# Unread identity matmuls in front of 48 TensorE steps at the start and the end of a 16-item pipeline

## The chip, the cores and the metric

The kernel runs on one core of one Trainium2 chip. The metric is device time in microseconds of one launch; the times given are medians of several launches on the same chip.

## The reference

The input has 16 items of 256 tokens by 256 features and a context of 77 rows for each item. A first layer is a transformer block: RMS norm and self-attention with 16 heads of 16 features, RMS norm and cross-attention to the context, RMS norm and a gated MLP with 1024 inner features.

```python
residual = hidden_states
h = rmsnorm(hidden_states, sa_norm_w)
h = residual + attention(h, h, sa_wq, sa_wk, sa_wv, sa_wo)
residual = h
hn = rmsnorm(h, ca_norm_w)
h = residual + attention(hn, context, ca_wq, ca_wk, ca_wv, ca_wo)
residual = h
hn = rmsnorm(h, mlp_norm_w)
h = residual + mlp(hn, w_gate, w_up, w_down)
```

A second layer takes the result `h` as queries: both `h` and the context are layer-normed, attention over the context with one head follows, then a GELU layer of 4 features and back to 256, a layer norm, self-attention over its 256 rows, and a sum with two learned scales.

## The kernel before, in words

All five engines run their own program. An item is cut into steps (`T.sa` transposes the normed tokens, `qk.sa` and `v.sa` make queries, keys and values, `S.sa.0` to `S.sa.7` the scores for the row maxima, `maxT.sa` transposes the maxima, `E.sa.0` to `E.sa.7` the scores shifted by them, `pv.sa.0` to `3` the attended values, `wo.sa` the projection; the same with `ca` for cross-attention; `T.mlp`, `gu.0` to `7` and `dnp.0` to `7` for the MLP; then `nFT`, `nXT`, `sc`, `pT`, `h4`, `xT`, `s2`, `mT2`, `e2`, `u2`, `fT`, `f2` for the second layer). Products whose operands are split in a high and a low part (`float32r`) run as three matmuls (`product`, line 1112); transposes, `pv`, `sc`, `h4` and `u2` have plain float32 operands.

`ORDER` writes out by hand the order in which each engine issues its steps, once around for each turn `it`; `name@a` stands for item `it + a`. `run` goes through the turns: the first and the last are unrolled, the middle ones are a hardware loop. The items overlap by up to four turns on TensorE, so that in the middle steps of several items stand between each other, and at the start and the end they don't. An engine issues strictly in this order. Where a step needs another engine's result, it waits for a semaphore. Steps that occur once (`kt`, `kg`, `fc`, weight splits `ws`) are in the same lists and do something only for item 0.

PSUM holds two tiles `ring` (attention), two `mring` (MLP and second layer), `od` (attended values) and `down_ps` (sum of the MLP, and before that scratch for `kt` and `kg`). The lines that matter here:

- TensorE (PE): `transposed` (L1120), `qk`, `v`, `wo`, `gu` by `product` (L1112), `scores` (L1173), `maxT` (L1180), `shifted` (L1193), `pv` (L1207), `dnp` (L1240), `t_nF` and `t_nX` (L1250), `sc` (L1269, L1271), `gram` (L1290, step `kg`), `pT` (L1298), `h4` (L1308), `t_sides` (L1316, step `xT`), `s2` (L1323), `mT2` (L1330), `e2` (L1337), `u2` (L1345), `t_stack` (L1352, step `fT`), `f2` (L1361).
- ScalarE (ACT): `scale_forms` (L693, L694, step `kg`) reads the Gram products from `down_ps` and writes `forms`; `mix_hi` (L676, step `fc`); `norm` (L723) squares the tokens and sums them; `exps` (L776).
- VectorE (DVE): the row maxima of the scores (L959, L964), the low parts (L937, L950, L952), `xn` (L932).
- GpSimd (POOL): `rstd` (L555) and, for each item, the chain of small operations that ends in `sides` (L650).
- SP issues the DMAs, among them those that pack queries and keys (`pk_sa<-qkT`, L493).

The first `dnp` of item 0 and `guard_forms` on VectorE wait until `forms` is made.

Of the kernel before, what the change touches and what calls it, by code (L numbers as in the profile page):

```python
# [23 lines left out]
P = 128  # L24
# [37 lines left out]
        xs@-6 hi.6@-5 hi.7@-5  # L62
    """,
    "act": """
        hi.7@-2 aT.ca@-1 v.sa@1 nXT@-2 norm.mlp@-1 h1@0 norm.ca@0 mT2@-3 ws.5@5 ws.10@1 T.mlp@-1 v.ca@0 T.ca@0 kg@0 e2@-3 maxT.sa@1 norm.sa@2 gu.0@-1 gu.1@-1
        qk.ca@0 hi.0@-1 E.sa.0@1 ws.7@4 gu.2@-1 hi.1@-1 E.sa.1@1 fc@4 E.sa.2@1 ws.4@6 gu.3@-1 nFT@-2 E.sa.3@1 fT@-3 E.sa.4@1 E.sa.5@1 sce@-2 ws.6@5 E.sa.6@1
        E.sa.7@1 pT@-2 ws.2@8 T.sa@2 hi.2@-1 hi.3@-1 maxT.ca@0 h4@-2 ws.3@7 ws.8@2 gu.4@-1 ws.0@15 qk.sa@2 cT.ca@1 gu.5@-1 E.ca.0@0 ws.9@2 hi.4@-1 hi.5@-1
        E.ca.1@0 gu.6@-1 ws.1@13 kt@12 aT.sa@1 gu.7@-1 E.ca.2@0 E.ca.3@0 hi.6@-1 xT@-2
    """,
# [34 lines left out]
def users(engine, wanted):  # L104

    return [(step, ahead) for step, ahead in STEPS[engine] if wanted(step)]


RINGS = {
# [35 lines left out]
def build(nc, x, ctx, w, vecs, norm_w, fc1t, fc1b, w5, out):  # L145
    st = ExitStack()
    with st:
# [941 lines left out]
        def _(pe):  # L1089
            mm = nc.tensor.matmul  # L1090
            pe.wait_ge(s_cset, 2)

            def weights(n, name):

                if at_first(n):
                    pe.wait_ge(s_wlo, C * (W_ORDER.index(name) + 1))
# [16 lines left out]
                return last  # L1113

            def transposed(n, tag):
                pe.wait_ge(S[tag, "xn"].sem, S[tag, "xn"].at(n, QT))
                ps = mfill(n, "T", "mlp") if tag == "mlp" else fill(n, "T", tag)[:, 0, :]
                for c in range(C):
                    for q in range(QT):
                        last = nc.tensor.transpose(ps[:, c * T + q * P:c * T + (q + 1) * P], XN[tag][:, q, c * P:(c + 1) * P], ident[:])  # L1120
                last.then_inc(S[tag, "T"].sem, 1)
# [6 lines left out]
                last.then_inc(S["cTmm"].sem, 1)  # L1128

            def qk(n, tag):  # L1130
                pe.wait_ge(S[tag, "lo"].sem, S[tag, "lo"].at(n, 1))
                if tag == "ca":
                    pe.wait_ge(S["cTlo"].sem, S["cTlo"].at(n, 1))
                    if at_first(n):
                        pe.wait_ge(s_cset, 10)
                weights(n, f"{tag}_wk")
                ps = fill(n, "qk", tag)
                wq, wk = wt[f"{tag}_wq"], wt[f"{tag}_wk"]
                src, kw = (hT_a, T) if tag == "sa" else (cT, SKV2)
                for m in range(C):  # L1140
                    product(ps[:, 0, m * T:(m + 1) * T], lambda a, kc: wq[a][:, kc, m * P:(m + 1) * P], lambda b, kc: hT_a[b][:, kc, :], C)
                for m in range(C):
                    last = product(ps[:, 1, m * kw:(m + 1) * kw], lambda a, kc: wk[a][:, kc, m * P:(m + 1) * P], lambda b, kc: src[b][:, kc, :], C)
                last.then_inc(S[tag, "qkmm"].sem, 1)

            def v(n, tag):
                if tag == "ca":
                    pe.wait_ge(S["cTlo"].sem, S["cTlo"].at(n, 1))
                weights(n, f"{tag}_wv")
                ps = fill(n, "v", tag)  # L1150
                wv = wt[f"{tag}_wv"]
                for q in range(QT if tag == "sa" else 1):
                    if tag == "sa":
                        last = product(ps[:, 0, q * D:(q + 1) * D], lambda a, kc: hT_a[a][:, kc, q * P:(q + 1) * P], lambda b, kc: wv[b][:, kc, :], C)
                    else:
                        last = product(ps[0:SKV, 0, 0:D], lambda a, kc: cT[a][:, kc, 0:SKV], lambda b, kc: wv[b][:, kc, :], C)
                last.then_inc(S[tag, "vmm"].sem, 1)

            def scores(n, tag, k):

                c, i0, pairs = pair_head(k, tag)
                if k == 0:
                    pe.wait_ge(S[tag, "pk0"].sem, S[tag, "pk0"].at(n, 16 * PACKS[tag][0]))
                if tag == "sa" and k == 4:
                    pe.wait_ge(S[tag, "pk1"].sem, S[tag, "pk1"].at(n, 16 * PACKS[tag][1]))
                ps = fill(n, "S", tag, k)
                kw = KW[tag]
                for i in range(pairs):
                    for q in range(QT):
                        for half in range(2):  # L1170
                            col = (i * QT + q) * kw
                            slot, r = SLOT_AT[tag](c, i0 + i), slice(HALF * half, HALF * half + MAX_ROW)
                            last = mm(ps[:, half, col:col + kw], qpk[tag][r, slot, q * P:(q + 1) * P], kpk[tag][r, slot, :], start=True, stop=True)  # L1173
                last.then_inc(S[tag, "S"].sem, 1)

            def maxT(n, tag):
                pe.wait_ge(S[tag, "nm"].sem, S[tag, "nm"].at(n, 1))
                ps = fill(n, "maxT", tag)
                for q in range(QT):
                    last = nc.tensor.transpose(ps[0:2 * SLOTS, 0, q * P:(q + 1) * P], nm[tag][:, q].rearrange("p h s -> p (h s)"), ident[:])  # L1180
                last.then_inc(S[tag, "maxT"].sem, 1)

            def shifted(n, tag, k):

                c, kt, i0, g = shifted_at(k, tag)
                if k == 0:
                    pe.wait_ge(S[tag, "mr"].sem, S[tag, "mr"].at(n, 16))
                ps = fill(n, "E", tag, k)
                rows_ = P if tag == "sa" else SKV
                for u in range(2):  # L1190
                    for half in range(2):
                        slot, r = SLOT_AT[tag](c, i0 + u), slice(HALF * half, HALF * (half + 1))
                        last = mm(ps[0:rows_, half, u * T:(u + 1) * T], kpk[tag][r, slot, kt * P:kt * P + rows_], qpk[tag][r, slot, :], start=True, stop=True)  # L1193
                last.then_inc(S[tag, "E"].sem, 1)

            def pv(n, tag, g):

                rows_, tiles = (P, QT) if tag == "sa" else (SKV, 1)
                c, kt = g // tiles, g % tiles
                pe.wait_ge(S[tag, "exp"].sem, S[tag, "exp"].at(n, 2 * (g + 1)))  # L1200
                if g == 0:
                    pe.wait_ge(S[tag, "vz"].sem, S[tag, "vz"].at(n, 1))
                if kt == 0:
                    reuse(pe, "od", ("pv", tag, g), n)
                for half in range(2):
                    for i in range(PAIRS):
                        last = mm(od[32 * i:32 * i + 32, half, :], vz[tag][0:rows_, kt, 8 * c + 2 * i + half, :], granule(g, tag)[0:rows_, i, half, :],  # L1207
                                  start=(kt == 0 and half == 0), stop=(kt == tiles - 1), tile_position=(0, 32 * i), skip_group_check=True)
                last.then_inc(S[tag, "pv"].sem, 1)

            def wo(n, tag):
                pe.wait_ge(S[tag, "athi"].sem, S[tag, "athi"].at(n, 1))
                pe.wait_ge(S[tag, "atlo"].sem, S[tag, "atlo"].at(n, 1))
                weights(n, f"{tag}_wo")
# [3 lines left out]
                last.then_inc(S[tag, "wo"].sem, 1)  # L1218

            def gu(n, m):  # L1220
                if m == 0:
                    pe.wait_ge(S["mlp", "lo"].sem, S["mlp", "lo"].at(n, 1))
                    weights(n, "up")
# [68 lines left out]
                    last.then_inc(s_gram, 1)  # L1292

            def pT(n):
                pe.wait_ge(S["lp"].sem, S["lp"].at(n, QT))
                ps = mfill(n, "pT")
                for q in range(QT):
# [1 line left out]
                last.then_inc(S["pTmm"].sem, 1)  # L1299

            def h4(n):
                pe.wait_ge(S["lpT"].sem, S["lpT"].at(n, 1))
                pe.wait_ge(S["xf"].sem, S["xf"].at(n, 1))
                if at_first(n):
# [4 lines left out]
                last.then_inc(S["h4"].sem, 1)  # L1309

            def t_sides(n):
                pe.wait_ge(S["xs"].sem, S["xs"].at(n, 7))
                ps = mfill(n, "xT")
                for side in range(2):
# [2 lines left out]
                last.then_inc(S["xT"].sem, 1)  # L1317

            def s2(n):
                pe.wait_ge(S["xTe"].sem, S["xTe"].at(n, 1))  # L1320
                ps = mfill(n, "s2")
                for q in range(QT):
# [1 line left out]
                last.then_inc(S["s2"].sem, 1)  # L1324

            def mT2(n):
                pe.wait_ge(S["smx"].sem, S["smx"].at(n, 1))
                ps = mfill(n, "mT2")
                for q in range(QT):
# [1 line left out]
                last.then_inc(S["mT2"].sem, 1)  # L1331

            def e2(n):
                pe.wait_ge(S["shift"].sem, S["shift"].at(n, 1))
                ps = mfill(n, "e2")
                for kt in range(QT):
# [59 lines left out]
```

## Time and profile before

| | us |
|---|---|
| median of 3 runs | 1021.01 (1020.12 to 1021.73) |
| the profiled execution | 1021.97 |
| its span, first to last instruction | 1020.2 |
| PE busy | 899.7 (88%), 8142 matmul records |
| DVE busy | 672.6 (66%) |
| ACT busy | 546.0 (54%) |
| POOL busy | 261.6 (26%) |
| chain that ended last, by engine | PE 77%, DVE 12%, issue 4%, ACT 3% |
| mean granted clock of TensorE | 0.937 |

Times in the profile are microseconds from the span's first instruction. PE is TensorE's matmuls, PEld its weight loads. `MATMUL ring<-hT_a_hi,sa_wq_hi` writes `ring` from the two operands; `128*128 128x256` has 128 rows and 128 columns of weights and 256 moving columns. A record's duration includes the way through the array, so neighbouring records overlap, and the distance from start to start is what one takes of the engine's time. In a merged row, the time runs from the first start to the last end.

### The profile page before, as it was taken

Reading aid. Unit: us, or ns where it says so; the run is one execution under the profiler, and the core shown is the slowest. Engines: PE = TensorE matmul, PEld = TensorE weight load, DVE = VectorE, ACT = ScalarE, POOL = GpSimd, SP = SyncE. Lnnn points to the kernel's source line nnn. Section 1 sums busy time; section 2 is a strip of 40 time slices with the busy share of each in tenths; the row PEclk is TensorE's granted clock in tenths of the full one; section 3 lists DMA queues with packets and bytes.
Section 4 is the critical chain, followed back from the end, with each engine's and each line's share of the span. In section 5 each row is a group of like instructions: output and inputs, shape, how many; then the busy total and the mean of one; then the engine's idle time right before and its main releaser. Section 6 shows DMA issues by size and latency. Waiting matters only on the chain.

```text
span 1020.2 us, 21920 instructions
## 1 busy us (share of the span) xinstructions
PE 899.7 (88%) x8142; PEld 762.2 (75%) x8142; DVE 672.6 (66%) x1439; ACT 546.0 (54%) x1129; POOL 261.6 (26%) x547
## 2 busy tenths in 40 slices
PE   3565879999999999999999999999999999989784
PEld 3434657788787888887878888788888787878673
DVE  4436284958677786959595867677685959564531
ACT  3332345455656657474656565655647475655342
POOL 7000001113232322222222323232322222233242
PEclk9766689999999999999999999999999999989895
DMA  6302121212222212021122221222213111201000
GB/s 186 120 13 75 53 79 53 80 52 69 64 77 66 77 59 85 26 97 44 54 80 64 80 63 66 65 76 65 76 28 106 33 59 63 65 4 53 4 11 21
DMA packets 69266, 63.97 MB, mean 63 GB/s; under 512 B 17280, under 2 KB 64496, under 8 KB 69184
## 3 DMA queue, kind: packets, MB, share of 16 engines
q1 hardware_dynamic: 69184, 62.87, 19.3%
q8 instruction: 53, 0.87, 0.4%
q14 instruction: 29, 0.24, 0.1%
HBM read 16.55 MB, written 4.19 MB: 20 GB/s over the span
## 4 chain that ended last, share of the span: by engine, by line
PE 77%; DVE 12%; issue 4%; ACT 3%; DMA 2%; POOL 1%; SPq 1%; DVEq 0%; POOLq 0%; ACTq 0%
PE mring L1112 18%; PE ring L1112 17%; PE down_ps L1240 10%; PE od L1207 10%; PE ring L1193 6%; PE ring L1173 6%; DVE mx_sa L959 5%; PE ring L1120 2%; DVE xn_a L932 2%; PE mring L1345 1%; PE mring L1269 1%; PE mring L1316 1%; PE mring L1308 1%; DVE xn_m L932 1%; DVE mx_ca L964 1%
## 5 line engine op out<-in xcount | busy, mean ns | idle before, releaser
L776 ACT ACTIVATE probs<-ring 128x1024 f32<-128x1024 f32 (+1 forms) x192 | 191.8, 1020 | 42.7 <-PE ring L1193 37.5
L559 POOL TENSOR_TENSOR hidT_lo<-hid,hidT_hi 128x256 fp32r<-128x256 f32 x128 | 94.7, 749 | 377.2 <-ACT hidT_hi L799 376.7
L959 DVE TENSOR_REDUCE mx_sa<-ring 128x4 f32<-128x1024 f32 x128 | 152.8, 1218 | 13.8 <-PE ring L1173 13.5
L1008 DVE SCALAR_TENSOR_TENSOR hid<-hid,mring 128x256 f32<-128x256 f32 x128 | 53.1, 415 | 90.8 <-ACT hid L791 90.4
L1173 PE MATMUL ring<-pk_sa 63*128 63x256 f32 x512 | 61.7, 341 | 27.7 <-DVE mx_sa L959 11.8
L1240 PE MATMUL down_ps<-down_hi,hidT_hi 128*128 128x256 f32 x256 | 80.0, 312 | 0.0
L1173 PEld LDWEIGHTS ring<-pk_sa 63*128 63x128 f32 x512 | 40.3, 201 | 47.1 <-DVE mx_sa L959 15.6
L975 DVE STREAM_TRANSPOSE oS<-od 128x512 f32<-128x512 f32 x64 | 45.7, 714 | 44.5 <-PE od L1207 43.9
L1207 PE MATMUL od<-probs,vz_sa 128*32 128x256 f32 x1024 | 72.0, 400 | 1.2 <-DVE oS L975 0.5
L1240 PE MATMUL down_ps<-down_lo,hidT_hi 128*128 128x256 f32 x256 | 72.6, 284 | 0.0
L1240 PE MATMUL down_ps<-down_hi,hidT_lo 128*128 128x256 f32 x256 | 72.5, 283 | 0.0
L791 ACT ACTIVATE hid<-mring 128x256 f32<-128x256 f32 x128 | 48.2, 380 | 40.6 <-PE mring L1112 39.6
L964 DVE TENSOR_REDUCE mx_ca<-ring 128x4 f32<-128x308 f32 x128 | 53.8, 474 | 18.2 <-PE ring L1173 16.8
L1193 PE MATMUL ring<-pk_sa 64*128 64x256 f32 x512 | 60.2, 335 | 5.3 <-DMA pk_sa<-mT 2.5
L799 ACT ACTIVATE hidT_hi<-hid 128x256 fp32r<-128x256 f32 x128 | 49.7, 410 | 28.1 <-PE down_ps L1240 27.2
L1112 PE MATMUL mring<-hT_m_hi,gate_hi 128*128 128x256 f32 x256 | 59.8, 316 | 2.4 <-DVE hT_m_lo L937 1.1
L950 DVE TENSOR_TENSOR qkT<-ring,qkT 128x512 fp32r<-128x512 f32 x32 | 22.1, 692 | 58.8 <-ACT qkT L749 58.8
L749 ACT ACTIVATE qkT<-ring 128x512 fp32r<-128x512 f32 x32 | 19.1, 598 | 72.1 <-PE ring L1112 72.1
L1193 PEld LDWEIGHTS ring<-pk_sa 64*128 64x128 f32 x512 | 39.5, 200 | 24.1 <-ACT probs L776 8.1
L1240 PEld LDWEIGHTS down_ps<-down_hi,hidT_hi 128*128 128x128 f32 x256 | 48.8, 191 | 10.9 <-POOL hidT_lo L559 6.2
L1010 DVE SCALAR_TENSOR_TENSOR hid<-hid,mring 128x256 f32<-128x256 f32 x128 | 53.9, 421 | 4.4
L732 ACT ACTIVATE hT_a_hi<-ring 128x512 fp32r<-128x512 f32 x32 | 19.1, 598 | 63.6 <-PE ring L1120 63.6
(278 smaller groups left out, 2424.6 us busy)
## 6 DMA issues: line engine op xcount, KB each, us to landing
pk_sa<-qkT SPq DMA_DIRECT2D x96, 256.0 KB, 2.7
qpk_ca<-qkT SPq DMA_DIRECT2D x48, 256.0 KB, 2.6
x_sb<-x SPq DMA_DIRECT2D x16, 256.0 KB, 2.8
x_res<-x SPq DMA_DIRECT2D x16, 256.0 KB, 2.7
out<-o_sb SPq DMA_DIRECT2D x16, 256.0 KB, 2.2
kpk_ca<-qkT SPq DMA_DIRECT2D x48, 78.0 KB, 2.1
ctx_sb<-ctx SPq DMA_DIRECT2D x16, 77.0 KB
ctx_l<-ctx SPq DMA_DIRECT2D x16, 77.0 KB
```

What stands on the lines that cost most here:

```text
L559: nc.gpsimd.tensor_tensor(hidT[1][:, m % HID, :], hid[:, m % 2, :], hidT[0][:, m % HID, :].bitcast(F32), ALU.subtract).then_inc(S["hidlo"] ...
L776: nc.scalar.activation(granule(g, tag)[0:rows_, i0:i0 + 2, :, :].rearrange("p i h t -> p h i t"), ring_tile(("E", tag, k))[0:rows_].rearra ...
L799: nc.scalar.activation(hidT[0][:, m % HID, :], hid[:, m % 2, :], ACT.Copy).then_inc(S["hidhi"].sem, 1)
L959: nc.vector.tensor_reduce(mx[tag][:, :, :, k].rearrange("p q h -> p h q"), ps[:].rearrange("p h (q t) -> p h q t", t=T), AX_X, ALU.max).th ...
L964: nc.vector.tensor_reduce(mx[tag][:, :, half, 2 * C * (k % 2) + k // 2:2 * C * (k % 2) + k // 2 + C + 1:C].rearrange("p q i -> p i q"), v, ...
L1008: nc.vector.scalar_tensor_tensor(out=hid[:, m % 2, :], in0=hid[:, m % 2, :], scalar=1.0, in1=ps[:, 0:T], op0=ALU.add, op1=ALU.mult).then_i ...
L1010: nc.vector.scalar_tensor_tensor(out=hid[:, m % 2, :], in0=hid[:, m % 2, :], scalar=0.5, in1=ps[:, T:2 * T], op0=ALU.mult, op1=ALU.mult).t ...
L1112: last = mm(outs, left(a, k % chunks), right(b, k % chunks), start=(k == 0), stop=(k == total - 1))
L1173: last = mm(ps[:, half, col:col + kw], qpk[tag][r, slot, q * P:(q + 1) * P], kpk[tag][r, slot, :], start=True, stop=True)
L1193: last = mm(ps[0:rows_, half, u * T:(u + 1) * T], kpk[tag][r, slot, kt * P:kt * P + rows_], qpk[tag][r, slot, :], start=True, stop=True)
L1207: last = mm(od[32 * i:32 * i + 32, half, :], vz[tag][0:rows_, kt, 8 * c + 2 * i + half, :], granule(g, tag)[0:rows_, i, half, :], start=(k ...
L1240: last = mm(down_ps[:, q, :], hidT[a][:, m % HID, q * P:(q + 1) * P], wt["down"][b][:, m, :], start=(m == 0 and q == 0 and k == 0), stop=( ...
```

## The change

`SPIN` is a table from a step and its item to a count. In front of each of these 48 steps, TensorE issues as many matmuls of the 128x128 float32 identity with itself; nothing reads the result. For items below 8 they write to the first 128 columns of `down_ps` and wait until `forms` is made; for the later items they write to `od` and wait until the last attended values are read. 310 of the 464 stand in front of 31 steps of items 0 to 2, 154 in front of 17 steps of items 13 to 15. Only unrolled turns hold them. The wait and the spins of a step come before the step's own wait. On ScalarE, `kg` moves from turn 0 to turn -4, right behind `fc`.

```diff
     "act": """
-        hi.7@-2 aT.ca@-1 v.sa@1 nXT@-2 norm.mlp@-1 h1@0 norm.ca@0 mT2@-3 ws.5@5 ws.10@1 T.mlp@-1 v.ca@0 T.ca@0 kg@0 e2@-3 maxT.sa@1 norm.sa@2 gu.0@-1 gu.1@-1
-        qk.ca@0 hi.0@-1 E.sa.0@1 ws.7@4 gu.2@-1 hi.1@-1 E.sa.1@1 fc@4 E.sa.2@1 ws.4@6 gu.3@-1 nFT@-2 E.sa.3@1 fT@-3 E.sa.4@1 E.sa.5@1 sce@-2 ws.6@5 E.sa.6@1
+        hi.7@-2 aT.ca@-1 v.sa@1 nXT@-2 norm.mlp@-1 h1@0 norm.ca@0 mT2@-3 ws.5@5 ws.10@1 T.mlp@-1 v.ca@0 T.ca@0 e2@-3 maxT.sa@1 norm.sa@2 gu.0@-1 gu.1@-1
+        qk.ca@0 hi.0@-1 E.sa.0@1 ws.7@4 gu.2@-1 hi.1@-1 E.sa.1@1 fc@4 kg@4 E.sa.2@1 ws.4@6 gu.3@-1 nFT@-2 E.sa.3@1 fT@-3 E.sa.4@1 E.sa.5@1 sce@-2 ws.6@5 E.sa.6@1
...
+SPIN = {
+    ("T.sa", 0): 19, ("qk.sa", 0): 11, ("S.sa.0", 0): 48, ("v.sa", 0): 16, ("S.sa.4", 0): 13, ("S.sa.6", 0): 7, ("S.sa.7", 0): 10,
+    ("maxT.sa", 0): 11, ("E.sa.0", 0): 19, ("E.sa.2", 0): 4, ("pv.sa.2", 0): 3, ("qk.sa", 1): 13, ("S.sa.0", 1): 39, ("wo.sa", 0): 7,
+    ("S.sa.4", 1): 13, ("S.sa.6", 1): 6, ("v.ca", 0): 2, ("maxT.sa", 1): 3, ("qk.ca", 0): 2, ("E.sa.1", 1): 6, ("E.sa.3", 1): 4,
+    ("S.ca.2", 0): 4, ("T.sa", 2): 3, ("qk.sa", 2): 6, ("E.ca.0", 0): 9, ("E.ca.2", 0): 6, ("E.ca.3", 0): 2, ("wo.ca", 0): 4, ("S.sa.6", 2): 4,
+    ("v.ca", 1): 5, ("S.ca.0", 1): 11, ("T.mlp", 15): 31, ("gu.0", 15): 7, ("gu.2", 15): 3, ("fT", 13): 6, ("pT", 14): 6, ("e2", 14): 7,
+    ("u2", 14): 10, ("fT", 14): 4, ("pT", 15): 4, ("h4", 15): 2, ("xT", 15): 43, ("s2", 15): 4, ("mT2", 15): 6, ("e2", 15): 3, ("u2", 15): 7,
+    ("fT", 15): 8, ("f2", 15): 3,
+}
...
+            def spin(n, *step):
+
+                count = SPIN.get((".".join(map(str, step)), n), 0) if isinstance(n, int) else 0
+                if count and n < B // 2:
+                    pe.wait_ge(s_form, 2)
+                elif count:
+                    pe.wait_ge(S["ca", "o"].sem, S["ca", "o"].at(B - 1, 2))
+                for _ in range(count):
+                    mm(down_ps[:, 0, 0:P] if n < B // 2 else od[:, 0, 0:P], ident[:], ident[:], start=True, stop=True)
...
             def transposed(n, tag):
+                spin(n, "T", tag)
                 pe.wait_ge(S[tag, "xn"].sem, S[tag, "xn"].at(n, QT))
```

The other step functions begin with the same call.

## Rows read from the trace of the kernel before

**Rows 1.** Page part 2: tenths in 40 slices of 25.5 us.

```profile
PE   3565879999999999999999999999999999989784
...
PEclk9766689999999999999999999999999999989895
```

**Rows 2.** Windows: stretch, its us, busy us (x instructions) of each engine, PEclk, DMA share, GB/s.

```profile
26.00:168.20 142.20, 99.08 (x717) 74.27 (x718) 70.65 (x109) 54.69 (x96) 6.08 (x9) 0.75 0.22 69
952.60:1016.90 64.30, 42.00 (x252) 36.85 (x252) 20.16 (x63) 23.02 (x52) 21.47 (x53) 0.74 0.03 10
```

**Rows 3.** Timeline of PE, three steps with long waits: start, us, work, [idle before <-releaser].

```profile
40.29 1.22 PE L1173 MATMUL ring<-pk_sa 63*128 63x256 f32 x8 [6.18 <-DMA pk_sa<-qkT]
...
956.58 1.11 PE L1120 MATMUL mring<-ident,xn_m 128*128 128x128 f32 x4 [4.01 <-DVE xn_m L932]
...
1005.26 1.12 PE L1316 MATMUL mring<-ident,sides 128*65 128x128 f32 x4 [5.47 <-POOL sides L650]
```

**Rows 4.** Timeline of PE, `qk` of items 0 and 1, line 1112.

```profile
29.21 0.63 PE L1112 MATMUL ring<-hT_a_lo,sa_wq_hi 128*128 128x256 f32 x2
...
33.48 0.63 PE L1112 MATMUL ring<-hT_a_hi,sa_wk_lo 128*128 128x256 f32 x2
...
73.62 0.41 PE L1112 MATMUL ring<-hT_a_lo,sa_wq_hi 128*128 128x256 f32 x2
...
76.00 0.40 PE L1112 MATMUL ring<-hT_a_hi,sa_wk_lo 128*128 128x256 f32 x2
```

**Rows 5.** Windows of seven stretches of the first part and three of the tail, with sums.

```profile
26.03:34.20 8.17, 6.57 (x28) 5.91 (x28) 0.69 (x1) 2.72 (x4) 0.00 (x0) 1.00 0.00 0
...
133.10:140.20 7.10, 7.10 (x52) 4.50 (x51) 6.03 (x8) 1.84 (x3) 0.00 (x0) 0.52 0.59 179
...
sum 80.67, PE 61.37 PEld 45.28 DVE 33.47 ACT 24.84 POOL 2.07; mean PE 8.77 PEld 6.47 DVE 4.78 ACT 3.55 POOL 0.30
...
sum 37.20, PE 22.42 PEld 18.74 DVE 6.97 ACT 12.70 POOL 9.01; mean PE 7.47 PEld 6.25 DVE 2.32 ACT 4.23 POOL 3.00
```

**Rows 6.** Groups by form, whole span (busy, mean ns); then timeline of one group each.

```profile
L1120 PE MATMUL ring<-ident,xn_a 128*128 128x128 f32 x128 | 22.4, 303 | 13.8 <-DVE xn_a L932 12.8 <-DVE mx_ca L964 0.6 <-ACT vz_ca L759 0.3
...
L1269 PE MATMUL mring<-nXT,nFT 128*128 128x77 f32 x128 | 17.3, 281 | 0.0
...
970.22 1.09 PE L1269 MATMUL mring<-nXT,nFT 128*128 128x77 f32 x8
...
312.21 0.60 PE L1120 MATMUL mring<-ident,xn_m 128*128 128x128 f32 x4
```

**Rows 7.** Timeline of PE and ScalarE at the start, and the forms' activation.

```profile
18.25 5.26 PE L1290 MATMUL down_ps<-w6T 128*128 128x5 f32 x24
26.03 1.11 PE L1120 MATMUL ring<-ident,xn_a 128*128 128x128 f32 x4 [2.51 <-DVE xn_a L932]
...
19.88 0.42 ACT L676 ACTIVATE mix<-o_sb 40x256 fp32r<-40x256 f32 x1 [2.31 <-POOL o_sb L601]
20.20 0.40 ACT L723 ACTIVATE xn_a<-x_sb 128x256 f32<-128x256 f32 x1
...
99.81 0.19 ACT L693 ACTIVATE forms<-down_ps 128x25 f32<-128x25 f32 x1
```

**Rows 8.** Timeline of PE around a rise and a fall of the clock.

```profile
66.52 1.93 PE L1207 MATMUL od<-probs,vz_sa 128*32 128x256 f32 x16
...
69.39 1.07 PE L1207 MATMUL od<-probs,vz_sa 128*32 128x256 f32 x16 [0.49 <-DVE oS L975]
...
84.72 0.77 PE L1112 MATMUL ring<-sa_wo_hi,atT_hi 128*128 128x256 f32 x2 [0.99 <-DVE mx_sa L959]
...
89.03 0.40 PE L1112 MATMUL ring<-sa_wv_lo,hT_a_hi 128*128 128x256 f32 x2
...
92.64 1.22 PE L1173 MATMUL ring<-pk_sa 63*128 63x256 f32 x8 [1.79 <-DVE mx_sa L959]
```

**Rows 9.** Page part 5: the exps of the softmax.

```profile
L776 ACT ACTIVATE probs<-ring 128x1024 f32<-128x1024 f32 (+1 forms) x192 | 191.8, 1020 | 42.7 <-PE ring L1193 37.5
```

More of the change, by code:

```diff
@@ L1130, in qk @@
             def qk(n, tag):
+                spin(n, "qk", tag)
                 pe.wait_ge(S[tag, "lo"].sem, S[tag, "lo"].at(n, 1))
@@ L1146, in v @@
             def v(n, tag):
+                spin(n, "v", tag)
                 if tag == "ca":
@@ L1159, in scores @@
             def scores(n, tag, k):
+                spin(n, "S", tag, k)
                 c, i0, pairs = pair_head(k, tag)
@@ L1176, in maxT @@
             def maxT(n, tag):
+                spin(n, "maxT", tag)
                 pe.wait_ge(S[tag, "nm"].sem, S[tag, "nm"].at(n, 1))
@@ L1183, in shifted @@
             def shifted(n, tag, k):
+                spin(n, "E", tag, k)
                 c, kt, i0, g = shifted_at(k, tag)
@@ L1211, in wo @@
             def wo(n, tag):
+                spin(n, "wo", tag)
                 pe.wait_ge(S[tag, "athi"].sem, S[tag, "athi"].at(n, 1))
@@ L1220, in gu @@
             def gu(n, m):
+                spin(n, "gu", m)
                 if m == 0:
@@ L1294, in pT @@
             def pT(n):
+                spin(n, "pT")
                 pe.wait_ge(S["lp"].sem, S["lp"].at(n, QT))
@@ L1301, in h4 @@
             def h4(n):
+                spin(n, "h4")
                 pe.wait_ge(S["lpT"].sem, S["lpT"].at(n, 1))
@@ L1311, in t_sides @@
             def t_sides(n):
+                spin(n, "xT")
                 pe.wait_ge(S["xs"].sem, S["xs"].at(n, 7))
@@ L1319, in s2 @@
             def s2(n):
+                spin(n, "s2")
                 pe.wait_ge(S["xTe"].sem, S["xTe"].at(n, 1))
@@ L1326, in mT2 @@
             def mT2(n):
+                spin(n, "mT2")
                 pe.wait_ge(S["smx"].sem, S["smx"].at(n, 1))
@@ L1333, in e2 @@
             def e2(n):
+                spin(n, "e2")
                 pe.wait_ge(S["shift"].sem, S["shift"].at(n, 1))
@@ L1340, in u2 @@
             def u2(n):
+                spin(n, "u2")
                 pe.wait_ge(S["sp2"].sem, S["sp2"].at(n, 1))
@@ L1348, in t_stack @@
             def t_stack(n):
+                spin(n, "fT")
                 pe.wait_ge(S["fs"].sem, S["fs"].at(n, 2))
@@ L1355, in f2 @@
             def f2(n):
+                spin(n, "f2")
                 if at_first(n):
```

1 line of the change is left out of this document (added).

## The prediction

> **What bounds the kernel now.** I read the page first, then the stretches by their sums, then TensorE's instructions in order of time. The page's 40 slices show TensorE (PE) busy for nine tenths or more in the middle, and less in the first six slices and in some of the last four, where the granted clock is lower too [rows 1]. PE is the engine that holds most of the chain that ended last. In between nothing changes by this diff, so the argument is about two stretches: from the first transpose of item 0 at 26.0 us to the first cross-attention scores of item 1 at 168.2 us, and from 952.6 us to the last matmul. PE is busy 99.08 of 142.2 us in the one and 42.00 of 64.3 us in the other, so it waits 43.1 and 22.3 us [rows 2]. The order of its steps is fixed, and its longest waits are 6.18 us for the packing DMAs of item 0, 5.47 for the GpSimd chain to `sides` of item 15 and 4.01 for `xn_m` [rows 3].
>
> The second loss is the clock. The column of the granted clock says 1.00 from 26.03 to 34.20 [rows 5], yet there 20 matmuls of 256 columns start 0.2135 us apart (29.21 to 33.48), and the same step for item 1 starts 20 of them in 2.38 us, 0.119 apart [rows 4]. The spacings are the two levels, 1.2 and 2.4 GHz; where column and spacing differ I go by the spacing. By it the level was low in seven stretches of the first part, with 61.37 us of busy PE, and in three of the tail, with 22.42 us [rows 5].
>
> **What a spin costs.** Each is a float32 matmul, 128x128 weights, 128 moving columns, not a transpose. Lines 1269 and 1120 tell what that makes: `sc` issues 4 such matmuls for each of 16 items and has 128 records, two for each; the transposes of line 1120 are 8 for each item and also have 128, one for each [rows 6]. So 464 spins are 928 records. Three rows bound one record at the high level. L1269 (weight load of 128 columns, short moving side) takes 1.09 us for 8: with a last one of 0.28 (the mean) that is 0.116 apart. Four transposes (128 moving columns, identity) take 0.60; with the same last one they are about 0.109 apart [rows 6]. L1112, which has a full load and as long a stream, gives 0.119 [rows 4]. I take 0.119 as a spin has both sides full: 0.238 us for a spin, 0.427 at the low level. The bounds are 0.218 and 0.238. This is what decides the case: the count in the table is the wait divided by half of that. `S.sa.0` of item 0 waited 6.18 us and gets 48 spins, `xT` of item 15 waited 5.47 and gets 43, `T.mlp` 4.01 and 31 [rows 3]: nine tenths of the wait at 0.115 to 0.116 each, one record. At 0.238 they take 11.4, 10.2 and 7.4 us. PE is in order, so what a spin takes beyond the wait delays the step.
>
> The Trainium skill (TensorE: Matmul & The Clock Gate, "Back-to-back issue gap") has about 81 ns for a sustained pair of load and matmul of 128 columns; by an estimate from that page a spin would be 0.162 us and the sum about 34 us lower. The float32 pairs of this trace do not agree with it, so the rows stand.
>
> **The sum, part by part.**
>
> *Forms moved up.* The first spin waits for the two activations of `forms`, which start at 99.81 us now, so the diff moves `kg` on ScalarE to just behind `fc` (19.88) and ahead of the norm of item 0 (20.20) [rows 7]. There it waits for the Gram products, which end at 23.51, and takes 0.3: the squares begin near 23.9, 3.7 later. Queued behind them are the mean square on VectorE, the power on GpSimd, `xn` and the transpose, which was at 26.03 and now could start at 29.7. Nothing else on ScalarE wants that time, and SP's and GpSimd's queues issue in the same order. PE meanwhile runs 19 spins from 24.0. At the low level all take 8.1 us (end 32.1), at the high 4.5 (end 28.5, the data then decide). The level had risen by 89.03, 4.3 us after the unbroken work of 84.72 had begun, but not in the 4.3 us from 29.21 to 33.48 [rows 4, 8]. I take the rise after 6 us: 14 low, 5 high, end 31.2. **+5.2** (bounds +3.7 and +6.1).
>
> *Clock.* From then on PE hardly pauses, and work that now runs low should run high: 61.37 us x (1 - 0.119/0.2135) = 0.443 gives **-27.2**, and in the tail 22.42 x 0.443 = **-9.9**.
>
> *Spins in place of waits.* In the first stretch 291 spins ahead of 30 steps (the 19 apart): 69.3 us, for 43.1 us of wait of which 2.0 stay as they are, so **+28.2**. In the tail 154 spins ahead of 17 steps: 36.7 for 22.0 of 22.3, **+14.7**.
>
> *Ends.* A step in front of a wait shows its last matmul in full, 0.28 against a spacing of 0.12 [rows 6]; a spin follows without that. 30 and 17 x 0.16: **-4.8** and **-2.7**.
>
> *New waits.* With PE faster, the exps at 1.02 us each [rows 9] set the pace of eight E steps of items 0 and 1, where PE has some 7.7 us of work and spins for 8.5 to 9; `S.sa.3` waits 0.5 for `vz`, and `maxT` of item 1 about 1 for its maximum. **+4**, and +0.5 in the tail (bounds 0 and 8). Packing DMAs and maxima stay under the spins: 11.4 us lie over the 6.18.
>
> Other additions: the waits on `s_form` and on `oS` of item 15 are met when reached (nothing, covered by program order); two writes to `down_ps` or `od` fall where these are free. 1,856 more records are instructions to fetch, none seen to stall PE: 0, at most 1.
>
> First stretch +5.4, tail +2.6, together **+8.0**. The middle is taken as unchanged, with up to 3 either way, since its few low stretches may fall otherwise. On the profiled execution (1021.97 around a span of 1020.2; 0.96 above the median) this is 1030.0; on the median 1021.01 it is **1029.0**.
>
> **Rivals.**
>
> *Cheap spins, the other side.* The gain of 44.6 us from clock and ends stands; only the price eats it. At 445 spins the break-even is 0.238 - 8.0/445 = 0.220 us. Place: the 48 in front of `S.sa.0` of item 0 and the 43 in front of `xT`. At 0.218 and with no new waits: 8.0 - 8.9 - 4.5 = -5.4, about 1015.6. For it: the transposes' stream is as long. Against: their weight load is shorter. 0.13. If a spin were one record, its time would fit the waits, spins would add nothing: start 3.7, -27.2 - 9.9 + 4.5 = -29, about 992. The record counts speak against it: 0.04. The page's 81 ns would give about 995; 0.02 for that.
>
> *Level falls in the thin parts.* It was high at 89.03 and low again by 92.64, with PE waiting 1.79 us just before [rows 8]. If the new waits near `maxT` of item 1 or in the E steps do that, two falls like the low stretch from 133.1 us, whose 7.10 us of work [rows 5] x 0.443 is 3.1, cost 6: 1035. 0.10.
>
> *The level does not rise for spins.* Then 445 x (0.427 - 0.238) = +84 and the 37 of gain are lost, and work that is now high turns low in part: above 1150. Against it, the rise between the two groups of `od` matmuls at 66.52 (1.93 us for 16) and 69.39 (1.07) came in the midst of float32 matmuls [rows 8]. 0.03. The Trainium skill (same page, Part 4) says that transposes by TensorE don't bring the full clock as they don't count as busy in the same way; a product of the identity with itself is computed as a plain matmul, and no row here shows one.
>
> *The diff does nothing,* its matmuls dropped as unread: no row speaks for it, under 0.01.
>
> **How the numbers follow.** Forecast's own case 0.56 (1023 to 1041), falls 0.10, no rise 0.03: slower 0.69. Within 2 us either way, where price and new waits lie between the bounds: 0.12. Cheap spins in their three forms: faster 0.19. 0.2%, 2 us, is about what a measurement of this kernel can tell from none. The range leaves out 992 to 995, the no-rise case and what lies beyond the outer bounds: 1014 to 1041.
>
> **What would show it.** Right: a spin group with two records for each, 0.237 us a spin; `S.sa.0` of item 0 preceded by 96 records over 11 us and no idle; `xT` of item 15 starting some 3 us later behind the last `h4` than now (5.47 to over 9.5); matmuls of L1112 at 0.119 from about 31 us on; item 0's transpose near 31; `forms` near 24. Wrong: 464 records, spins of 0.12, PE idle ahead of the spun steps, or spacings of 0.2135 in the midst of them.

## The result, and the profile after

The changed kernel takes 1028.16 us (median of 20 runs, 1027.51 to 1030.21), the kernel before on the same chip 1022.97 (20 runs, 1018.96 to 1027.77). The ratio is 1.0047, 95% interval 1.0032 to 1.0061: slower, by about half a per cent. The forecast was 1029.0. The profiled execution has a span of 1026.4 us against 1020.2, 6.2 longer.

The page of the changed kernel, parts 1 and 2 (cut), answers to [rows 1]:

```profile
PE 968.4 (94%) x9070; PEld 841.2 (82%) x9070; DVE 672.0 (65%) x1439; ACT 545.2 (53%) x1129; POOL 261.5 (25%) x547
...
PE   4999999999999999999999999999999999989998
...
PEclk9999999999999999999999999999999999999999
```

Every slice but the first and two near the end is now nine tenths full, and the mean granted clock is 0.992, for 0.937 before: what is left at the low level is TensorE's work up to 27.7 us (by its spacings; the column shows 1.00 there) and five short stretches in the middle. By busy share and clock this looks like an ideal kernel, and it is slower than before. What fills the waits of both ends is line 1112, the spins. Their instructions in the changed kernel (durations are min/median/max):

```profile
L1112 PE MATMUL down_ps<-ident x620: 270/275/579, 24.1 to 174.2; 128*128 128x128 f32 x155
...
L1112 PE MATMUL od<-ident x308: 270/275/357, 957.2 to 1022.4; 128*128 128x128 f32 x154
```

620 + 308 = 928 records for 464 spins: two for each. The windows of the changed kernel, from the first transpose of item 0 to the first cross-attention scores of item 1, and from the first `smax` transpose of the tail's first step to the end of the last matmul (columns as in [rows 2]; there the tail's window begins behind the same `smax` step, which starts at 952.19 in the kernel before and has 0.38 us of work):

```profile
30.13:174.39 144.26, 139.60 (x1301) 121.75 (x1300) 70.34 (x109) 53.89 (x94) 6.08 (x9) 1.00 0.22 69
...
957.02:1022.98 65.96, 65.58 (x565) 63.88 (x563) 20.41 (x63) 23.20 (x52) 21.41 (x53) 1.00 0.03 11
```

The waits are nearly gone: 144.26 - 139.60 = 4.66 us are left in the first stretch and 0.38 in the tail, for 43.1 and 22.3 before [rows 2]. Yet both stretches are longer. TensorE in order of time, changed kernel:

```profile
24.09 6.20 PE L1112 MATMUL down_ps<-ident 128*128 128x128 f32 x38 [0.37 <-ACT forms L705]
30.13 0.60 PE L1142 MATMUL ring<-ident,xn_a 128*128 128x128 f32 x4
...
35.63 0.40 PE L1133 MATMUL ring<-hT_a_hi,sa_wk_lo 128*128 128x256 f32 x2
35.86 10.88 PE L1112 MATMUL down_ps<-ident 128*128 128x128 f32 x96
46.67 0.73 PE L1198 MATMUL ring<-pk_sa 63*128 63x256 f32 x8
47.33 3.84 PE L1112 MATMUL down_ps<-ident 128*128 128x128 f32 x32
...
53.71 3.17 PE L1112 MATMUL down_ps<-ident 128*128 128x128 f32 x26
56.81 0.74 PE L1198 MATMUL ring<-pk_sa 63*128 63x256 f32 x8
...
957.24 7.08 PE L1112 MATMUL od<-ident 128*128 128x128 f32 x62
964.16 0.60 PE L1142 MATMUL mring<-ident,xn_m 128*128 128x128 f32 x4
...
1003.40 9.85 PE L1112 MATMUL od<-ident 128*128 128x128 f32 x86
1013.08 0.60 PE L1349 MATMUL mring<-ident,sides 128*65 128x128 f32 x4
```

`S.sa.0` of item 0 waited 6.18 us; now 96 records stand there for 10.8. `T.mlp` waited 4.01 and has 6.9 in its place; `xT` waited 5.47 and has 9.7 [rows 3]. No bracket with a releaser stands behind the steps that follow: their data were there before the spins ended. 95 spacings in 10.88 - 0.28 us are 0.112 each, so within a group a spin costs 0.223 us, against 0.115 in the table's sizes. A short group costs more: the 13 spins from 53.71 to 56.81 take 3.10 us, 0.238 each. Record by record, where a group stands behind matmuls with 63 or 64 rows or 32 columns of weights (23 of the 30 in the first stretch), the last of these keeps TensorE for 0.2 us or more before the first spin's record starts, and that record for 0.213.

The ledger, from the starts of the same steps in both traces:

| stretch | forecast | measured | of which |
|---|---|---|---|
| start, to `T.sa` of item 0 | +5.2 | +4.1 | 26.03 to 30.13 |
| first stretch | +0.2 | +2.1 | work -28.1, spins for waits +30.2 |
| middle | 0, 3 either way | -1.4 | |
| tail | +2.6 | +1.4 | work -11.5, spins for waits +12.9 |
| sum | +8.0 | +6.2 | |

To divide a stretch, each matmul record counts from its start to the start of the next one, or to its own end where TensorE then idles. In the first stretch the 582 spin records behind the first 38 count 68.7 us (0.236 for each spin); the waits fell by 43.1 - 4.66 = 38.4, which leaves +30.2. The rest of busy TensorE is 139.60 - 68.7 = 70.9, for 99.1 before. In the tail, 308 records count 34.7 us (0.226 for each spin) in place of 21.8 us of waits (22.2 - 0.4), and the rest fell from 42.4 to 30.8.

So two large terms of opposite sign stand against each other, and three theories could be had from the start. **Theory P (price):** the clock and the filled waits are worth some 25 to 35 us; each spin costs two records where the counts assume one, and that eats it all. **Rival R (no gain to have):** the spins bring nothing, or the moved forms are what costs. **Rival T:** what a spin must be, to hold the clock, is a plain matmul.

### The profile page after: what moved, and what is told of

Same layout as the page of the kernel before. It is cut to its first block, busy times and chain, and to the rows that moved or that the text cites. A ratio compares the mean times of both kernels' runs of the same rounds, so it can differ in the third digit from the quotient of the medians.

```text
span 1026.4 us, 23776 instructions
## 1 busy us (share of the span) xinstructions
PE 968.4 (94%) x9070; PEld 841.2 (82%) x9070; DVE 672.0 (65%) x1439; ACT 545.2 (53%) x1129; POOL 261.5 (25%) x547
## 4 chain that ended last, share of the span: by engine, by line
PE 86%; DVE 8%; issue 2%; ACT 1%; DMA 0%; POOL 0%; SPq 0%; DVEq 0%; ACTq 0%; POOLq 0%
PE mring L1133 19%; PE ring L1133 16%; PE down_ps L1270 10%; PE od L1235 9%; PE down_ps L1112 7%; PE ring L1220 6%; PE ring L1198 5%; DVE mx_sa L970 4%; PE od L1112 3%; PE ring L1142 2%; PE mring L1382 1%; PE mring L1299 1%; DVE xn_a L943 1%; PE down_ps L1320 1%; PE mring L1349 1%
## 5 line engine op out<-in xcount | busy, mean ns | idle before, releaser
L1112 PE MATMUL down_ps<-ident 128*128 128x128 f32 x620 | 78.4, 283 | 0.4 <-ACT forms L705 0.4
L1112 PEld LDWEIGHTS down_ps<-ident 128*128 128x128 f32 x620 | 73.3, 196 | 4.1 <-issue 1.2
L1235 PE MATMUL od<-probs,vz_sa 128*32 128x256 f32 x1024 | 68.5, 385 | 0.7
L1198 PE MATMUL ring<-pk_sa 63*128 63x256 f32 x512 | 57.9, 323 | 9.8 <-DVE h L1013 4.1
L1198 PEld LDWEIGHTS ring<-pk_sa 63*128 63x128 f32 x512 | 37.4, 187 | 27.5 <-DVE mx_sa L970 10.7
L1220 PE MATMUL ring<-pk_sa 64*128 64x256 f32 x512 | 57.2, 322 | 1.0 <-ACT probs L787 1.0
```

Of the source, the lines that this page charges most:

```text
L1112: mm(down_ps[:, 0, 0:P] if n < B // 2 else od[:, 0, 0:P], ident[:], ident[:], start=True, stop=True)
```

## The experiments

Each edit is against the changed kernel, and none changes what is computed. Each ratio is to runs of the kernel before on the same chip. `kg_only`, `half`, `transposes` and `half_kg2` ran on one chip; `two_halved`, `half_up`, `tail_only` and `early_spins` on a second; `half_shifted` and `early_19` on a third; `kg2_shifted` on a fourth. Between chips the ratios are the fairer comparison, and a difference of medians is only a rough one.

**The move of `kg` alone.** `SPIN` is emptied; the order on ScalarE is the changed one.

```diff
-SPIN = {
-    ("T.sa", 0): 19, ("qk.sa", 0): 11, ...
-}
+SPIN = {}
```

> The changed kernel with an empty SPIN table: only kg stands earlier on ScalarE. Theory (the price of the spins makes the loss, the early kg a part of it): the squares of item 0 begin 3.7 us later and the whole pipeline with them, so 2 to 4 us over the kernel before, clock low in the same places. Rival (the late start is hidden by the weight splits or DMAs): within 1 us of before.

Measured: 1024.36 us (12 runs), before 1021.82 (17 runs), ratio 1.0021, interval 0.9998 to 1.0044. The interval just reaches 1, so a loss in time is not settled by it. The delay at the start is in the timeline of TensorE:

```profile
29.67 1.12 PE L1134 MATMUL ring<-ident,xn_a 128*128 128x128 f32 x4 [5.66 <-DVE xn_a L935]
```

The transpose stood at 26.03 with a wait of 2.51 [rows 7] and stands at 29.67: 3.6 later, which is the 3.7 worked out for the squares queued behind `kg`. The span of this one execution is 2.3 longer; if that holds for the kernel, about 1.3 is made up later, but executions of one kernel differ by more than that. The other 0.5 of the changed kernel's 4.1 is the first spin group, which outlasts the data.

**Half the spins.** One edit tests the price: counts that a spin of 0.223 fills.

```diff
-                for _ in range(count):
+                for _ in range(count // 2):
```

> Each count of SPIN halved and rounded down, so that a group of records takes nine tenths of its wait at 0.113 us a record. Theory (a spin is two records of 0.113, what goes beyond the wait is the loss, and the clock's gain is whole): the 464 spins took 104 us in place of some 65 us of waits, so about 39 us less than the changed kernel, 2 of it lost to waits that come back: 991, between 985 and 998. Rival (the clock stays high only because the spins leave no gap): low stretches come back, 1000 to 1012. Rival (the loss has little to do with the price): above 1018.

Measured: 1001.18 us (4 runs), ratio 0.9789 (0.9759 to 0.982). Windows of this kernel, the first stretch and 7.7 us inside it:

```profile
105.80:113.50 7.70, 7.70 (x56) 5.90 (x55) 4.16 (x11) 1.02 (x1) 0.00 (x0) 0.50 0.00 0
29.11:155.96 126.85, 113.25 (x993) 91.79 (x994) 70.15 (x109) 53.95 (x94) 6.08 (x9) 0.96 0.24 78
```

The same spins, half as many, are worth 2.1% against before and some 26 us against the changed kernel (by the ratios 1.0047 and 0.9789). Rival R falls. But the gain is 10 us short of the 991 expected, and 1001.18 lies where the rival of returning low stretches was put (1000 to 1012). One such stretch is there: 7.70 us at the low level in the first window. What stands in front of it, on TensorE in this kernel:

```profile
104.95 0.92 PE L1198 MATMUL ring<-kpk_ca,qpk_ca 63*128 63x78 f32 x8 [1.92 <-DMA qpk_ca<-qkT]
105.80 1.93 PE L1235 MATMUL od<-probs,vz_sa 128*32 128x256 f32 x16
```

A wait of 1.92 us for a packing DMA, then the low clock. Two suspects for the missing 10 us follow: this wait with what hangs on it (1.92 and 7.70 x 0.443 = 3.4 us), and the waits that a count rounded down leaves open (126.85 - 113.25 = 13.6 us of idle in all). A third thing stands in the same window. Counted as above, TensorE's own work in the stretch is 74.3 us, for 99.1 before, but the waits, with the spins in them, are 39.0 + 13.6 = 52.6 us, for 43.1 before: the data come from other engines and DMAs, which did not get faster (VectorE is busy for 70.15 us in the window, 70.65 before), so part of what the clock saves turns into wait.

**Transposes in place of matmuls,** full counts: same operands, one record for each.

```diff
-                    mm(down_ps[:, 0, 0:P] if n < B // 2 else od[:, 0, 0:P], ident[:], ident[:], start=True, stop=True)
+                    nc.tensor.transpose(down_ps[:, 0, 0:P] if n < B // 2 else od[:, 0, 0:P], ident[:], ident[:])
```

> The full counts, but each spin a transpose of the identity (one record of 0.109 us) in place of a float32 matmul. Theory (TensorE's clock follows transposes as it follows matmuls): the same as the halved counts within 4 us, about 991. Rival, from the Trainium skill (TensorE: Matmul & The Clock Gate, Part 4: transposes don't bring the full clock): spacings of 0.2135 stay where they were low before, each spin takes 0.21 and 97 us of spins stand against 65 of waits: 1040 to 1060.

Measured: 997.41 us (4 runs), ratio 0.9755 (0.9724 to 0.9785). The spins and the steps behind them in this kernel:

```profile
24.07 4.32 PE L1112 MATMUL down_ps<-ident 128*128 128x128 f32 x19 [0.37 <-ACT forms L705]
29.36 0.66 PE L1142 MATMUL ring<-ident,xn_a 128*128 128x128 f32 x4 [0.97 <-DVE xn_a L943]
29.85 1.36 PE L1112 MATMUL down_ps<-ident 128*128 128x128 f32 x11
...
31.83 0.39 PE L1133 MATMUL ring<-hT_a_lo,sa_wq_hi 128*128 128x256 f32 x2
...
29.35:151.30 121.95, 109.15 (x1009) 86.84 (x1009) 70.07 (x109) 54.09 (x94) 6.08 (x9) 1.00 0.25 81
```

Nineteen spins are 19 records here, spaced by 0.109 at the high level, and the `qk` matmuls of item 0 run at the high level from 31.52 us, where they ran at the low one before [rows 4]. The change as it was sized fits this instruction. Rival T falls: a transpose brings and holds the high level as well. The same division of the first stretch into TensorE's work and its waits, for five kernels:

| us | length | work | spins | idle | spins and idle |
|---|---|---|---|---|---|
| before | 142.2 | 99.1 | 0 | 43.1 | 43.1 |
| changed kernel | 144.3 | 70.9 | 68.7 | 4.7 | 73.3 |
| `half` | 126.9 | 74.3 | 39.0 | 13.6 | 52.6 |
| `transposes` | 121.9 | 71.2 | 37.9 | 12.8 | 50.7 |
| `half_shifted` (below) | 121.8 | 71.2 | 38.0 | 12.7 | 50.7 |

The clock, with what the ends of the groups give, saves 28 us of work in three of them. Where the spins fit, 7.6 us of that come back as longer waits, and 20 are kept; in the changed kernel 30 come back.

**Half, with `kg` in another place:** behind the squares of item 0, so that they don't queue behind it.

```diff
-... fc@4 kg@4 E.sa.2@1 ...
+... fc@4 E.sa.2@1 ...
-... norm.sa@2 gu.0@-1 ...
+... norm.sa@2 kg@2 gu.0@-1 ...
```

> Halved counts and kg on ScalarE right behind the norm of item 0 (turn -2) rather than ahead of it. Theory (the late squares cost at the start): the first transpose comes near 27 in place of 30, and the whole is 2 to 4 us under the halved counts alone, about 988. Rival (start hidden): equal to it within 1 us.

Measured: 999.82 us (4 runs), ratio 0.9767 (0.9736 to 0.9798), 1.4 under `half` on the same chip, with ranges that just don't overlap. Less than expected: the transpose moved only from 29.11 to 28.10, since now the 18 records ahead of it hold it, and the wait of the cross-attention scores was there again, at 2.04 us, with low stretches from 60.4 and 108.2 us in this execution.

**The two largest counts alone:** 48 to 24 and 43 to 21.

```diff
-    ... ("S.sa.0", 0): 48, ...
+    ... ("S.sa.0", 0): 24, ...
-    ... ("xT", 15): 43, ...
+    ... ("xT", 15): 21, ...
```

> The changed kernel with only two counts cut: 48 to 24 ahead of S.sa.0 of item 0 and 43 to 21 ahead of xT of item 15. Theory (what one group takes beyond its wait goes to the end undiminished): 24 x 0.224 = 5.4 less 0.8 of wait that comes back, and 22 x 0.224 = 4.9 less 0.9: 8.6 under the changed kernel, 1019.6. Rival (an overrun is caught up by later slack): under 4 us.

Measured: 1020.78 us (12 runs), ratio 0.9987 (0.997 to 1.0005); 7.4 under the changed kernel by the medians and 6.1 by the ratios, for 8.6 expected. On TensorE in this kernel:

```profile
37.07 5.52 PE L1112 MATMUL down_ps<-ident 128*128 128x128 f32 x48
43.43 0.74 PE L1198 MATMUL ring<-pk_sa 63*128 63x256 f32 x8 [0.83 <-DMA pk_sa<-qkT]
...
1007.50 4.93 PE L1112 MATMUL od<-ident 128*128 128x128 f32 x42
1013.36 0.65 PE L1349 MATMUL mring<-ident,sides 128*65 128x128 f32 x4 [0.92 <-POOL sides L661]
```

The steps behind the spins have their releasers back, 0.83 us for the packing DMA and 0.92 for `sides`: the spins now end just ahead of the data. The traced execution is the slowest of the twelve, though (1028.48 us): its cross-attention scores of item 0 waited 1.60 us for a packing DMA, and a low stretch of 10.2 us followed. The two groups can be read from it, the total can't. 46 fewer of 464 spins turn the change from slower into no measurable difference. This is the most direct evidence for theory P.

**The tail alone,** with transposes as spins and `kg` back in its old turn (these two edits not shown).

```diff
-                count = SPIN.get(...) if isinstance(n, int) else 0
+                count = 0 if isinstance(n, int) and n < B // 2 else SPIN.get(...) if isinstance(n, int) else 0
```

> Transposes as spins only ahead of the 17 steps of the tail, kg back in its old turn. Theory: the first stretch as before, the tail 7.4 us shorter as in the run with transposes everywhere (57.2 against 64.6): about 1014.5 against 1022. Rival (the gains of the two ends are not independent): more than 2 us away from that.

Measured: 1014.07 us (10 runs), ratio 0.9946 (0.9918 to 0.9973). As expected: the tail alone gives 5.5 us (by the ratio) to 6.6 (by the medians) of the 24 of `transposes`.

**Half, rounded up.** The question was whether the short waits that rounding down leaves open matter, and whether the wait at 105 us returns.

```diff
-                for _ in range(count):
+                for _ in range((count + 1) // 2):
```

> Halved counts rounded up rather than down: 19 more matmuls in all, which also moves the 16 KB blocks in which TensorE's instructions are fetched. Theory (in the halved counts the packing DMAs of item 0's cross-attention landed after 4.4 us in place of 2.6 because such a block came at the same moment, at 101.6 us; the 1.92 us of wait let the clock fall for some 7 us): if the block falls elsewhere, the wait ahead of the first S.ca is 0.4 and the time 3 to 4 us less than the halved counts: 998. Rival (the wait belongs to the halved counts, whatever the blocks do): 1001 to 1003, the same wait of 1.9.

Measured: 997.81 us (4 runs), ratio 0.977 (0.9732 to 0.9807), 3.4 under `half` by the medians and 1.9 by the ratios, whose intervals overlap. In its trace the 1.92 us are gone:

```profile
104.36 0.64 PE L1198 MATMUL ring<-kpk_ca,qpk_ca 63*128 63x78 f32 x8 [0.35 <-ACT probs L787]
```

**What made that wait.** The DMAs that pack `qpk_ca` for item 0, in `half` and in `half_up`, from issue to landing:

```profile
DMA to landing us min/median/max: 2.9/3.1/4.4
...
q8 instruction: 1, 0.02, 0.8%
```

```profile
DMA to landing us min/median/max: 2.5/2.6/2.7
```

The second line of the first fence is from the queues of `half` between 99 and 106 us: one packet of the queue that fetches instructions, 16 KB, while the three packing DMAs are on their way. In `half_up` the same window has no such line. In four kernels (`half`, `half_kg2`, `two_halved`, `early_spins`) such a packet fell 1 to 2 us behind the last of the three issues, and the wait was 1.60 to 2.04 us; in the six others with spins in this stretch none fell there, and the wait was 0.34 or 0.35. To move only the packet, 24 unread matmuls were put ahead of TensorE's first step, where it waits anyway:

```diff
             pe.wait_ge(s_cset, 2)
+            for _ in range(24):
+                mm(down_ps[:, 0, 0:P], ident[:], ident[:], start=True, stop=True)
...
-                for _ in range(count):
+                for _ in range(count // 2):
```

> The halved counts (rounded down) with 24 more matmuls of the identity ahead of TensorE's first step, where it waits until 12.9 us anyway. They do nothing for the places of the waits, but they move TensorE's program by 96 instructions, 6 KB, so the 16 KB block that was fetched at 101.6 us comes some 5 us earlier. Theory (that block delayed the packing DMAs): the wait ahead of the first S.ca goes from 1.9 to 0.4 us and the low stretch behind it is gone: 997 to 998 in place of 1001.2. Rival (rounding up helped by its spins, the block is chance): wait 1.9, 1001.

Measured: 996.82 us (4 runs), ratio 0.9779 (0.9755 to 0.9802), before 1020.18. On TensorE:

```profile
103.78 0.64 PE L1200 MATMUL ring<-kpk_ca,qpk_ca 63*128 63x78 f32 x8 [0.34 <-ACT probs L787]
```

With the counts of `half`, the wait is gone and the median is 4.4 us lower, on another chip; by the ratios it is 1.0, which is not clear of noise. The trace is the surer witness: no packet falls among the three DMAs, and the first stretch is 121.8 us long for 126.9, 5.0 shorter, where the wait and the low stretch were priced at 5.3. `half_up`, with 122.9, is no shorter than this, so rounding down costs nothing here. So some kernels of this family carry up to 5 us in the first stretch that go with where their instruction blocks fall.

**Spins from the start.** On top of `transposes`, 70 more ahead of the first step, and 50 ahead of `T.sa` of item 0, were to bring the high level before the Gram products.

```diff
             pe.wait_ge(s_cset, 2)
+            for _ in range(70):
+                nc.tensor.transpose(down_ps[:, 0, 0:P], ident[:], ident[:])
...
-    ("T.sa", 0): 19, ...
+    ("T.sa", 0): 50, ...
```

> Transposes as spins, and 70 more before TensorE's first step, while it waits for the 12.9 us of masks and folding, and 50 in place of 19 ahead of T.sa of item 0. Theory (the early kg costs 3.3 us at the start because the Gram products run at the low clock until 23.5 and the squares wait for them): with the clock up they end near 18.9, before the squares are due at 20.2, so T.sa of item 0 starts near 26.1 as in the kernel before, 3.3 us under the run with transposes: 994. Rival (the clock falls during the Gram products, whose moving side has 5 columns): spacings of 0.2135 in them, T.sa near 29.5, the same time as with transposes.

Measured: 1002.53 us (4 runs), ratio 0.9802 (0.9761 to 0.9844): 8 us worse than expected, and 5 worse than `transposes`. The start in this kernel:

```profile
1.55 10.37 PE L1104 MATMUL down_ps<-ident 128*128 128x128 f32 x70 [1.55 <-POOL ident L536]
...
14.19 2.39 PE L1322 MATMUL down_ps<-wcT 128*128 128x5 f32 x20 [0.67 <-ACT w6T L697]
16.44 4.77 PE L1322 MATMUL down_ps<-w6T 128*128 128x5 f32 x24
21.58 8.41 PE L1114 MATMUL down_ps<-ident 128*128 128x128 f32 x50 [0.37 <-ACT forms L705]
29.83 0.60 PE L1144 MATMUL ring<-ident,xn_a 128*128 128x128 f32 x4
```

At the low level 70 records would take 69 x 0.2135 + 0.28 = 15.0 us; they took 10.37, so the level rose in the midst of transposes alone. It was still high for the first 20 Gram products (2.39 us) and fell among the next 24 (4.77 us, for 5.26 at the low level [rows 7]); the column of the granted clock has the rise at 6.74 and the fall at 16.98. The 50 spins then ran at the low level for most of their 8.41 us, and held the transpose to 29.83. What was gained in the forms was lost behind them, and the cross-attention scores of item 0 waited 1.98 us for their packing DMA again, with an instruction packet behind the issues.

The same with 19 in front of `T.sa` again:

```diff
-    ("T.sa", 0): 50, ...
+    ("T.sa", 0): 19, ...
```

> As early_spins, with 19 again in place of 50 transposes ahead of T.sa of item 0. There the forms were made at 21.6 us, and the 50 ran at the low clock until 29.8. Theory: 19 at 0.2135 end at 25.7, T.sa starts near 26.2, 3.2 us before that of the run with transposes (29.4): 994, and up to 4 more if an instruction block meets the packing DMAs of item 0. Rival (the start is bound by the norm behind the early kg all the same, forms at 21.3 against squares due at 20.2): T.sa near 27.5, 996.

Measured: 1002.19 us (4 runs), ratio 0.982 (0.9792 to 0.9849). Missed as well. In this execution the Gram products took the low level from the first (20 in 4.12 us), and:

```profile
42.66 1.23 PE L1200 MATMUL ring<-pk_sa 63*128 63x256 f32 x8 [2.79 <-DMA pk_sa<-qkT]
```

An instruction packet fell at 38.0 us, among the packing DMAs of `pk_sa`; the wait is 2.79 us, with a low stretch behind it, where it is 0.94 in `transposes`.

**Both changes together.** `half_shifted`, with `kg` behind the squares and 4 spins in place of 9 ahead of the first transpose.

```diff
-    ("T.sa", 0): 19, ...
+    ("T.sa", 0): 8, ...
-... fc@4 kg@4 E.sa.2@1 ...
+... fc@4 E.sa.2@1 ...
-... norm.sa@2 gu.0@-1 ...
+... norm.sa@2 kg@2 gu.0@-1 ...
```

> As half_shifted, with kg behind the norm of item 0 (turn -2) and 4 matmuls in place of 9 ahead of T.sa of item 0. In half_kg2 the norm was no longer late, but T.sa still started at 28.1, as 9 spins at the low clock stood ahead of it. Theory: 4 spins end at 25.9, T.sa starts near 26.1, 3.4 us earlier than in half_shifted, of which qk of item 0 gives back 1 to 1.5 at the low clock: 995. Rival (the earlier start brings an instruction block onto a packing DMA, or is caught up by the DMAs): 997 to 1001.

Measured: **995.19 us** (6 runs, 994.78 to 997.67), before 1021.67, ratio 0.9734 (0.9708 to 0.976). As expected. The start:

```profile
23.85 2.08 PE L1114 MATMUL down_ps<-ident 128*128 128x128 f32 x8 [0.37 <-ACT forms L705]
26.19 1.12 PE L1144 MATMUL ring<-ident,xn_a 128*128 128x128 f32 x4 [0.27 <-DVE xn_a L943]
```

The transpose is back at 26.19, 0.16 from where it was before [rows 7], and the gain is 2.7% with about half of the spins. It is the lowest ratio of all, but its interval overlaps those of `transposes` and `half_shifted`, and the span of its traced execution is that of `transposes` (993.5 and 993.6), so a lead over these is not shown.

## Why the prediction was right

By its own steps:

- **Two records for each spin.** Right: 928 for 464. This was the step that decided the sign, read from two counts in a trace that had no such instruction [rows 6].
- **0.238 us a spin.** Right in the first stretch (0.236, start to start), but for another reason: within a group it is 0.223, nearer to the spacing of L1269 (0.116) and below both float32 rows, so "both sides full" doesn't hold, and the changeovers at the groups' edges make up the rest. In the tail, where all groups but one stand behind matmuls with 128 rows, it was 0.226. The estimate of 0.162 from the Trainium skill (TensorE: Matmul & The Clock Gate, "Back-to-back issue gap") was further off, and the trace does not agree with it.
- **Clock, -27.2 and -9.9.** Right, with one misreading. The stretch from 40.2 to 68.4 was counted as low throughout, but in the midst of it eight scores took 0.76 us, where the eight at 40.29 took 1.22 [rows 3]. The line, and a window around it with a granted clock of 0.96, in the kernel before:

```profile
49.80 0.76 PE L1173 MATMUL ring<-pk_sa 63*128 63x256 f32 x8 [1.79 <-DVE mx_sa L959]
...
49.70:51.50 1.80, 0.76 (x8) 0.57 (x8) 1.14 (x2) 0.00 (x0) 0.00 (x0) 0.96 0.00 0
```

  That is under 2 of the 61.37 us. Pairing the same records of both traces, the low ones that don't stand in front of a wait fell from 52.1 to 29.6 us in the first stretch, a factor of 0.43, and from 15.5 to 8.4 in the tail, 0.46, around the forecast's 0.443. With this factor for those in front of a wait, the clock is worth some 26 and 9 us.
- **Ends, -4.8 and -2.7.** This is the mis-sized term of the gain. Work fell by 28.1 and 11.5 us in all, so only some 2.0 and 2.3 are left for the ends. The forecast took the last matmul in front of a spin to cost 0.12; it costs 0.2 in front of most groups of the first stretch.
- **The sum.** Clock and ends were forecast at -44.6 and came to -39.6; spins and new waits at +47.4 and came to +43.1. The two errors, 5.0 and 4.3, nearly cancelled.
- **Start, +5.2.** +4.1. The queueing on ScalarE was right (3.6 of 3.7 in the run without spins, `forms` at 23.76 for 23.9). The step that was off is the rise of the level, taken after 6 us of spins: 38 records in 6.20 us, with 0.28 for the last, are (5.92 - 37 x 0.1116) / (0.2135 - 0.1116) = 18 at the low level, some 3.8 us (the column of the granted clock has the rise at 27.68, 3.6 us after the first spin). It differs between kernels: the 70 transposes of `early_spins` give (10.09 - 69 x 0.109) / 0.1045 = 25, some 5.3 us.
- **New waits, +4 and +0.5.** 4.66 us of idle are left in all, for some 6 forecast: right in kind, slightly high.
- **Tail, +2.6.** +1.4: the ends gave 0.4 less, the clock 0.7 less, and spins and waits took 2.3 less. **Middle:** -1.4, inside its 3.
- **Rivals.** The cheap spins came true within a group (0.223, between 0.218 and 0.238), but not over the first stretch as a whole (0.236), and not in the time. Level falls in the thin parts: none in the changed kernel, whose granted clock is 1.00 in both stretches; but `half` had one of 7.70 us behind a wait of 1.92, so the mechanism is there; whether the surplus of spins is what kept it away was not tried. No rise for spins: fallen. The Trainium skill (TensorE: Matmul & The Clock Gate, Part 4) has it that transposes don't bring the full clock; the traces do not agree: 70 transposes alone raised it in `early_spins`, and `transposes` held it, at a mean of 0.990 in the traced execution and 997.4 us.

The forecast's own time was close partly by luck: two errors of 4 to 5 us, nearly as large as the whole 6.2, had opposite signs. That what a spin takes beyond a wait goes to the end is shown by `two_halved` (6.1 to 7.4 of 8.6) and `half`. How the gain divides between clock and ends is worked out from the paired records and was not tried apart by a run.

## What to carry to other kernels

Filling TensorE's waits with unread work to hold its clock pays here (2.7% of the kernel), but each filler costs what it issues: count its records before sizing it, and fit it to end just ahead of the data, where the releaser of the next step is still to be seen. A page that shows every slice full at the full clock is no proof of speed, if part of what fills it is filler. Don't expect the clock's gain in full: as TensorE gets faster, its waits for the others grow, here by 7.6 of 28 us. And when the instruction stream is shifted, look again at the waits for small DMAs: 5 us of the first stretch came and went with an instruction packet.

## What the runs showed of the hardware that was not expected

- A transpose of the identity holds and raises the clock like a matmul, at 0.109 us a record, and its weight load takes 0.140 us where that of the float32 matmul takes 0.192 (medians of line 1112 in both kernels). Whether that is why the matmul's record takes 0.1116 and the transpose's 0.109 was not tried.
- Going from matmuls with 63 or 64 rows of weights to 128x128 ones costs at the high level: the spacings around the change are 0.2 and 0.213 us, for 0.112 within the group.
- The clock fell in the midst of 44 back-to-back Gram products with 5 moving columns, from 0.11 us a product to about 0.2 (4.77 for 24). In `early_19`, which idled 2.61 us ahead of them, for 1.27, they took the low level from the first. What the idle time and what the products did was not told apart.
- A 16 KB instruction packet next to packing DMAs goes with landings of up to 4.5 us (`qpk_ca` in `half_kg2`, `pk_sa` in `early_19`); without one, the three of `qpk_ca` for item 0 land within 2.7 in every kernel. `half_shifted` moved the packet by edit and the wait went; through what the two meet (a ring, a port, memory) stays open.
- Runs of before spread over 8.8 us (1018.96 to 1027.77), those of the changed kernel over 2.7. The clock goes with it: of the 54 runs of before beside the experiments, the nine above 1025.5 us had a mean granted clock of 0.927 to 0.932, the other 45 of 0.931 to 0.938. What sets off the slower ones was not tried.
